# Two transformer-like layers on one core: the long convolution's transforms regrouped by batch and by parity of time, and the bias tables in one buffer

## The reference

```python
xz = einsum('bld,ed->bel', hidden_states, W_in); x, z = split(xz, 2, axis=1)
x  = silu(conv_b + sum_j conv_w[:, j] * xp[:, :, j:j + Lq])      # 4 taps, 256 channels
y  = irfft(rfft(x, 2*Lq) * rfft(k_ssm, 2*Lq))[..., :Lq]          # k_ssm has 512 taps
y  = (y + x * D_skip) * silu(z)
out = einsum('bhl,dh->bld', y, W_out)
...
ctrl = einsum('th,tho->to', hidden, w2) + b2                     # b2 = expert_b2[chosen expert]
```

## Time and profile before

| | |
|---|---|
| three executions | 460.07, 460.67, 460.44 us, median 460.44 |
| the profiled execution | 460.52 us |
| its span, first to last instruction | 458.7 us |
| mean granted TensorE clock | 0.969 |
| PE busy | 420.9 us (92%) |
| PE weight loads busy | 211.1 us (46%) |
| DVE busy | 330.3 us (72%) |
| ACT busy | 190.6 us (42%) |
| DMA moved | 7.27 MB, mean 16 GB/s |

### The profile page before, as it was taken

The page is one execution under the profiler, slowest core; times in us unless marked ns, Lnnn a source line. Parts: engine busy times, 40 slices in busy tenths (PEclk is TensorE's granted clock), DMA queues, the critical chain, the costliest instruction groups (busy, mean ns, idle before and its releaser), DMA issues.

```text
span 458.7 us, 4175 instructions
## 1 busy us (share of the span) xinstructions
PE 420.9 (92%) x1398; PEld 211.1 (46%) x1398; DVE 330.3 (72%) x680; ACT 190.6 (42%) x314; POOL 21.8 (5%) x37
## 2 busy tenths in 40 slices
PE   4792987979999999999999999999999999999992
PEld 1341564655765365344644443433734433343361
DVE  4999898889973994597988674695553863274565
ACT  1343568443136412446143445344037526324441
POOL 0010203011000000000000000000000000000001
PEclk9896999979999999999999999999999999999997
DMA  6300000040000000000000000000000000000001
GB/s 220 150 1 0 1 1 0 2 149 2 1 0 1 1 0 0 1 0 1 1 1 0 1 0 23 0 1 1 0 1 0 24 0 1 1 0 0 1 0 46
DMA packets 5148, 7.27 MB, mean 16 GB/s; under 512 B 1075, under 2 KB 4232, under 8 KB 4872
## 3 DMA queue, kind: packets, MB, share of 16 engines
q1 hardware_dynamic: 3968, 4.80, 3.0%
q10 hardware_dynamic: 1160, 2.21, 1.4%
HBM read 5.95 MB, written 1.05 MB: 15 GB/s over the span
## 4 chain that ended last, share of the span: by engine, by line
PE 72%; DVE 6%; ACT 3%; issue 1%; POOL 1%; POOLq 0%; DVEq 0%
PE ring L1239 23%; PE ring L1217 8%; PE ring L1234 5%; PE timebank L274 5%; PE bankA L200 4%; PE ring L1219 4%; PE specbank L262 3%; PE ring L1247 3%; PE ring L1254 2%; PE ring L1258 2%; PE bankA L274 2%; PE ring L1261 2%; PE bankA L262 1%; PE ring L1265 1%; PE ring L1256 1%; PE ring L1262 1%
## 5 line engine op out<-in xcount | busy, mean ns | idle before, releaser
L1239 PE MATMUL ring<-hm,wc 128*128 128x512 f32 (+1 forms) x252 | 108.6, 581 | 0.0
L1239 PEld LDWEIGHTS ring<-hm,wc 128*128 128x128 f32 x252 | 46.1, 190 | 61.0 <-issue 52.8
L1445 DVE SCALAR_TENSOR_TENSOR hm<-xtm,cst,h 128x512 f32<-128x512 bf16 x48 | 33.4, 747 | 6.0 <-ACT h L1353 6.0
L200 PE MATMUL bankA<-wconv,h2w 128*128 128x256 f32 x128 | 34.9, 423 | 0.0
L1367 ACT ACTIVATE gts<-ring 128x512 f32<-128x512 f32 (+1 forms) x18 | 9.9, 550 | 52.3 <-PE ring L1239 52.3
L1353 ACT ACTIVATE h<-ring,vec 128x512 f32<-128x512 f32 x32 | 21.9, 687 | 17.0 <-PE ring L1219 14.9
L200 PEld LDWEIGHTS bankA<-wconv,h2w 128*128 128x128 f32 x128 | 25.7, 210 | 5.6 <-issue 2.0
L1534 DVE SCALAR_TENSOR_TENSOR f2e<-hl,f2e 128x512 f32<-128x512 f32 (+1 forms) x9 | 5.7, 632 | 27.2 <-ACT hl L1398 27.2
L1234 PE MATMUL ring<-hm,wc 64*128 64x512 f32 (+1 forms) x84 | 22.9, 621 | 0.4 <-DVE hm L1445 0.4
L1364 ACT ACT_TABLE_LOAD x8 | 10.3, 1283 | 28.4 <-PE ring L1239 28.4
L274 PE MATMUL timebank<-cst,abc 128*128 128x256 f32 x96 | 21.2, 379 | 0.0
(11 more groups left out here) (264 smaller groups left out, 762.5 us busy)
## 6 DMA issues: line engine op xcount, KB each, us to landing
wc<-in_w_c SPq DMA_DIRECT2D x1, 1664.0 KB
cst<-in_const ACTq DMA_DIRECT2D x1, 1096.0 KB
out<-xall SPq DMA_DIRECT2D x8, 128.0 KB, 1.9
wc<-in_x_feat SPq DMA_DIRECT2D x1, 768.0 KB, 13.0
bconv<-in_bcast SPq DMA_DIRECT2D x1, 512.0 KB, 7.6
wc<-in_k_time ACTq DMA_DIRECT2D x1, 512.0 KB
wc<-in_x_feat ACTq DMA_DIRECT2D x1, 256.0 KB, 3.7
wa<-in_w_a SPq DMA_DIRECT2D x1, 256.0 KB, 3.5
```

What stands on the lines that cost most here:

```text
L200: ins = pe.matmul(at, h2w[:, n, h * P + tap:h * P + tap + P], wconv[:, tap, :], start=False, stop=(h == HALVES - 1 and tap == TAPS - 1))
L1239: ins = pe.matmul(dst[:, at], wc[:, w:w + P], hm[:, seat(j, made + g - 1), at], start=False, stop=(g == PAIRS - 1))
L1445: dve.scalar_tensor_tensor(hm[:, seat(j, k), :], picked, cst[:, C_EG + g:C_EG + g + 1], h[:, g, :], ALU.is_equal, ALU.mult).then_inc(S["hm ...
```

## The change

1. **Forward unit.** It is now one batch and the whole spectrum. Time is split by parity (even and odd times) and not in halves; `h2w`, the window that feeds the short convolution, is stored by parity for it. The low frequencies (even numbers e = 0) and the mirrored ones (e = 1) share blocks of cosines and sines up to a sign, so the constant table shrinks from 2192 to 1677 columns. A unit is 8 products of 256 columns.
2. **Inverse unit.** Its output is also by parity: 16 products of 128 columns in place of 8 of 256. `gate` puts the two parities back in order of time as it reads `zs` and writes `ys`.
3. **Products on DVE.** The same elements for one batch and the whole spectrum. Two explicit waits on DVE's own earlier results (`Z_ready`) are added.
4. **Lists that are empty.** `FOLDED` and `UNFOLDED` are empty tuples, so `keep_odd`, the branch in `spectra` and those in `products_now` and `inverse_half` issue nothing.
5. **Bias tables.** One float32 buffer of 88 rows of 384 holds the experts' bias twice (rows 0 to 23 and 64 to 87) and the convolution's at rows 32 to 34. It is loaded by one transfer and split once, at the start. The second split, the copy by DMA and PE's wait for it are gone.
6. **Small moves.** `project_gate` reads `h2T` and not the window, so the window's copy no longer waits for the gates' products. The filter is loaded in rows of 512 elements. POOL sets the ones.

```diff
         def forward_half(pe, c, b, bank, ahead=0):
-            after(pe, prod_done, 2 * c + e - ahead)
-            for ri in range(2):
-                for kh in range(HALVES):
-                    ins = pe.matmul(banks[ri][:, :].rearrange("p (b c) -> p b c", b=BATCH), cst[:, C_FWD + kh * 2 * WIN + (2 * ri + e) * P:][:, 0:P],
-                                    xtm[:, c, kh:kh + HALVES + 1:HALVES, :], start=(kh == 0), stop=(kh == HALVES - 1))
+            after(pe, prod_done, 2 * c + b - ahead)
+            for e in range(2):
+                for ri in range(2):
+                    at = bank[:, e, ri * INNER:(ri + 1) * INNER]
...
+                    for par in range(2):
+                        ins = pe.matmul(at, block_of(C_FWD, par, e, ri), xtm[:, c, b * HALVES + par, :], start=(par == 0), stop=(par == 1))
             ins.then_inc(fwd_done, 1)
...
         def inverse_half(pe, c, cc, dst):
             pe.wait_ge(Z_ready, 4 * (c + 1))
             for b in range(BATCH):
-                for e in range(2):
-                    for ri in range(2):
-                        ins = pe.matmul(dst[:, b * WIN:(b + 1) * WIN], z[:, e, at, b * INNER + cc * P:b * INNER + (cc + 1) * P],
-                                        cst[:, C_INV + (2 * ri + e) * WIN:][:, 0:WIN], start=(e == 0 and ri == 0), stop=(e == 1 and ri == 1))
+                for par in range(2):
+                    at = dst[:, (2 * b + par) * P:(2 * b + par + 1) * P]
...
+                    for e in range(2):
+                        for ri in range(2):
+                            ins = pe.matmul(at, z[:, e, ri if c == 0 else 1 - ri, cols], block_of(C_INV, par, e, ri),
+                                            start=(e == 0 and ri == 0), stop=(e == 1 and ri == 1))
...
         def products_late(dve, c, b, bank):
+            dve.wait_ge(Z_ready, 2 * (2 * c + b + 1))
+            after(dve, inv_done, CC * c)
...
         def gate(dve, c, cc, src):
             dve.wait_ge(inv_done, CC * c + cc + 1)
-            dve.tensor_tensor(ys[:, cc, :], src[:, :], zs[:, c, cc, :], ALU.mult).then_inc(gate_done, 1)
+            timed = lambda a: a.rearrange("p (b s a) -> p b a s", b=BATCH, a=2)
+            dve.tensor_tensor(timed(ys[:, cc, :]), src[:, :].rearrange("p (b a s) -> p b a s", b=BATCH, a=2), timed(zs[:, c, cc, :]), ALU.mult).then_inc(gate_done, 1)
...
                 act.dma_start(hT[:, :, 1:1 + WIN], x_feat[:, :, 0:WIN]).then_inc(first_in, 16)
-                act.dma_start(cstb[:, :], consts).then_inc(consts_in, 16)
-                act.dma_start(rowf[:, :], rows.partition_broadcast(3)).then_inc(row_in, 16)
-                for part in range(3):
-                    act.dma_start(bef[part * EXPERTS:(part + 1) * EXPERTS, :], biasE).then_inc(consts_in, 16)
-                act.dma_start(kt[:, :, :], k_time.rearrange("(b p) c -> p b c", p=P)).then_inc(b_in, 16)
+                act.dma_start(biasf[:, :], biases).then_inc(row_in, 16)
+                act.dma_start(kt.rearrange("p (d a) c -> p d (a c)", a=2), k_time.rearrange("(d p a) c -> p d (a c)", p=P, a=2)).then_inc(b_in, 16)
...
-                        after(act, piece_done, (c - 2) * PIECES)
-                        act.activation(h2w[:, :, :], h2T[:, :, ds((c - 2) * WIN, TAPS - 1 + WIN)], ACT.Copy).then_inc(window_placed, 1)
+                        if c > 2:
+                            act.wait_ge(piece_done, (c - 3) * PIECES + BATCH)
+                        act.activation(h2w[:, :, :, :], h2T[:, :, ds((c - 2) * WIN, TAPS + WIN)].rearrange("p b (i q) -> p b q i", q=2), ACT.Copy).then_inc(window_placed, 1)
...
                         rounded(c - 1)
-                        split(bef[:, :], be2split[0:3 * EXPERTS, :], cst[:, C_PM:C_PM + 3], late_split)
                         residual_end(c - 1)
...
-                sp.wait_ge(late_split, 1)
-                sp.dma_start(be2split[HID:HID + 3 * EXPERTS, :], be2split[0:3 * EXPERTS, :]).then_inc(S["biases_doubled"], 16)
```

More of the change, by code:

```diff
@@ L111, in constants @@
     c[:, C_E24] = EXPERTS - np.arange(P) % EXPERTS
-    c[:, C_RANK:C_PM] = EXPERTS - np.arange(EXPERTS)
-    for part in range(3):
[L114 to L117, removed]
+    c[:, C_RANK:C_ALL] = EXPERTS - np.arange(EXPERTS)
+    return c
 class Steps:
@@ L175, in after, with two_layers @@
         eng.wait_ge(sem, count)
-def two_layers(nc, x_tok, x_feat, vecs, bias8, rows, bcast, biasE, w_a, w_b, k_time, d_skip, w_c, w64, w32, const, consts, out):
+def two_layers(nc, x_tok, x_feat, vecs, bias8, bcast, biases, w_a, w_b, k_time, d_skip, w_c, w64, w32, const, out):
     ds = bass.ds
@@ L255, in two_layers @@
         bsteps = Steps(None, b_steps)
[L257 to L264 removed]
+        part = lambda c, b: abc[:, c % 3, :, :, b * INNER:(b + 1) * INNER]
@@ L300, in products_now @@
+        def products_now(dve, c, b, bank, between=None, ready=False):
+            s = bsteps
+            s.eng = dve
+            if not ready:
+                spectra(dve, c, b, bank)
+            xr, xi = real(bank), imag(bank)
+            now, last = part(c, b), part(c - 1, b)
+            after(dve, Z_ready, 2 * (2 * c + b))
+            after(dve, b_steps, s.base + s.n)
             if c == 0:
-                s.go(dve.tensor_tensor(both(now), x2(xr), taps2(e, 0), ALU.mult))
+                s.go(dve.tensor_tensor(now, x2(xr), taps2(0), ALU.mult))
@@ L327, in products_late @@
-        def products_late(dve, c, e, banks):
+            if c == 0 and c not in UNFOLDED:
+                dve.tensor_tensor(now[:, :, 0, :], now[:, :, 0, :], tt[:, :, 0, :], ALU.subtract).then_inc(Z_ready, 1)
+                dve.tensor_tensor(now[:, :, 1, :], now[:, :, 1, :], tt[:, :, 1, :], ALU.add).then_inc(Z_ready, 1)
+                return
+            s.go(dve.tensor_tensor(now[:, :, 0, :], now[:, :, 0, :], tt[:, :, 0, :], ALU.subtract))
+            s.link(dve.tensor_tensor(now[:, :, 1, :], now[:, :, 1, :], tt[:, :, 1, :], ALU.add))
@@ new lines, in products_now @@
+            if c not in UNFOLDED:
+                dve.wait_ge(inv_done, CC * c)
+                dve.tensor_tensor(last[:, :, 1, :], now[:, :, 0, :], last[:, :, 1, :], ALU.subtract).then_inc(Z_ready, 1)
+                dve.tensor_tensor(last[:, :, 0, :], now[:, :, 1, :], last[:, :, 0, :], ALU.add).then_inc(Z_ready, 1)
+                return
+            whole = now
+            if c > 0:
+                whole = tt
+                s.go(dve.tensor_tensor(tt[:, :, 0, :], now[:, :, 0, :], last[:, :, 1, :], ALU.subtract))
+                s.link(dve.tensor_tensor(tt[:, :, 1, :], now[:, :, 1, :], last[:, :, 0, :], ALU.add))
@@ L329, in products_late @@
+            dve.tensor_tensor(last[:, 0, :, :], whole[:, 0, :, :], whole[:, 1, :, :], ALU.add).then_inc(Z_ready, 1)
+            dve.tensor_tensor(last[:, 1, :, :], whole[:, 0, :, :], whole[:, 1, :, :], ALU.subtract).then_inc(Z_ready, 1)
+        def products_late(dve, c, b, bank):
             if c == CHUNKS - 1:
@@ L944, in two_layers @@
             ring3, ring0 = psum("ring3"), psum("ring0")
-            Xb = [psum(f"specbank{i}") for i in range(2)]
             ring1, ring2 = psum("ring1"), psum("ring2")
@@ L1670, in col @@
         return c
+    biases, masks = np.zeros((R_ALL, CTRL), np.float32), np.zeros((R_ALL, 3), np.float32)
+    for part in range(3):
+        for at in (part * EXPERTS, HID + part * EXPERTS):
+            biases[at:at + EXPERTS], masks[at:at + EXPERTS, part] = f["e_expert_b2"], 1.0
+        biases[R_CONV + part, 0:INNER], masks[R_CONV + part, part] = f["m_conv_b"].ravel(), 1.0
     vecs = np.concatenate([col(f["a_time_decay"]), col(f["a_time_first"]), col(f["a_time_mix_key"]), col(f["a_time_mix_value"]),
```

238 lines of the change are left out of this document (130 added, 108 removed).

## The result

The changed kernel takes 461.55 us (median of ten runs, 460.67 to 461.99) against 460.14 us for the kernel before in the same rounds (ten, 459.24 to 460.67). The ratio is 1.0032, interval 1.0022 to 1.0042: 1.4 us slower. The prediction was 461.5 us.

A forecast was written before the change was run, and what follows sets the result against it. The prediction took DVE's chain as the bound up to some 96 us and PE's stream after. 0.84 + 0.17 + 0.1 = +1.1 us on the profiled 460.52 us, less 0.08 us to the median, gave 461.5 us; range 460.3 to 463.2 us.

The forecast's parts named there:

- Inverse units: Eight units on PE's path, each 32 records of 128 columns at 111 ns instead of 16 of 256: +0.84 us.
- longer runs do not hold 111 ns: Rival: PE's longer runs of 128 columns are slower; at 130 ns a record 4.9 us more, 466.4 us; chance 0.05.
- every load uncovered: Rival: 192 ns for each of PE's added weight loads is paid in full, +36.9 us, 498 us; chance 0.01.
- Forward units: Seven units on PE's path, each 16 records of 256 columns instead of 8 of 512: +0.17 us.
- The likeliest rival: No change: 0.20 us at the head of five forward units goes, 460.5 us; chance 0.30, smaller terms included.
- Products on DVE: Same elements per instruction, new waits hidden under PE's stream: 0, or 6 x 0.1 us if uncovered.
- Transfers at the start: The 135 KB bias table competes with `wa`, which starts everything: +0.1 us, between 0 and 0.35.
- the table gets in the way of `wa`: Rival at the start: table delays `wa` or lands after 6.9 us; further +0.3 to +0.5 us, 461.9 us; chance 0.12.
- First split grown: DVE's split at the start grows from 3.06 to 3.82 us, with 0.67 us left before `ksb`: cost 0.
- Gates, window's copy: Steps over every second float32 cost 0; rival that they cost double, +1.5 us, 463.0 us, chance 0.10.
- Second split removed: DVE's 3.82 us from 105.17 us go, but PE, busy from 95.86 us on, does not wait there: gain 0.
- Slow stretch: PE's clock 0.50 from 96 us stays; rival that it goes saves about 3.2 us, 458.3 us, chance 0.05.

The follow-up runs named there:

- experiment 1: Changed kernel with its inverse products back at 256 columns, both parities side by side: 460.67 us, ratio 1.0019 to the kernel before.
- experiment 4: Kernel before with each inverse product of 256 columns cut into two of 128: 461.14 us, ratio 1.0024.
- Experiment 7: Kernel before with each inverse product of 256 columns cut into four of 64: 489.69 us, ratio 1.0637.
- experiment 5: Changed kernel with two unread float32 products of 512 columns keeping PE busy in turn 4: 460.51 us, ratio 1.0004 to the kernel before.
- experiment 6: Kernel before with two unread float32 products of 512 columns keeping PE busy in turn 4: 459.20 us, ratio 0.9981.
- experiment 11: Changed kernel with 256-column inverse products, bias table behind `wa` on SyncE's queue, two unread PE products in turn 4: 458.59 us, ratio 0.9974 to the kernel before.
- experiment 8: Changed kernel with the second split's eight DVE instructions back in turn 4, result unused: 462.17 us, ratio 1.0041 to the kernel before.
- experiment 3: Changed kernel with the bias table behind `wa` on SyncE's queue and the filter waiting for `wa`: 461.29 us, ratio 1.0029 to the kernel before.
- experiment 12: As experiment 11, plus seven unread products of 512 columns on PE in turn 1: 458.06 us, ratio 0.9957 to the kernel before.

## Why the prediction was right, and where it wasn't

- **Inverse units** (forecast +0.84): +0.93 us by the four pairs, 0.23 each. Right; the mechanism, a record's price by its width on PE's path, is shown by experiments 1 and 4 from both sides. The 111 ns of the 16-record row hold for 64 and 128 records. The rival "longer runs do not hold 111 ns" is out, and so is every load uncovered: the trace does not bear out the strict reading of the overlap rule that the prediction weighed. Experiment 7 adds what the prediction did not know: of 256, 128 and 64 columns, 128 is the narrowest that is still nearly free. The Trainium skill's page "TensorE: Matmul & The Clock Gate" (LDWEIGHTS) gives a load by its columns alone, divided by 1.2 per ns; as an estimate by that, 107 ns for 128. The float32 floor of 111 ns agrees within 4%; the bf16 row at 55 ns a record is shorter than this formula gives.
- **Forward units** (+0.17): +0.02 each, +0.12 us. Right, but the prediction counted seven on the path and five behind products of a part of the array; the chain of both kernels has six and four. The likeliest rival, that the 0.20 us at the head of five units would go, did not happen: 3.65 against 3.45 us.
- **Products on DVE** (0): right. From the first complex product of turn 4 to the end of the rounding, where all of it is in the chain, DVE takes 10.2 us in experiment 5 (94.17 to 104.33) and in experiment 6 (95.36 to 105.51), so the regrouping and its waits cost nothing there.
- **Transfers at the start** (+0.1, stated bounds 0 and 0.35): 0.45 us in the first profile, 0.21 to 0.74 us in six profiles with the table beside `wa`, four of them above 0.35. **This is the term that failed**, and its upper bound with it. The prediction priced 135 KB at the best rate in sight, 389 GB/s, and hoped that most of it would fall behind `wa`. The rates of the windows do not bear out a sum of bytes: by 5.0 us the engines had moved only some 68 KB more than before (699 against 631 KB, each window's rate by its 0.5 us), though `wa` landed 0.45 us later, and from 3.0 to 3.5 us they moved less, at 158 and not 285 GB/s. In experiment 11, with the table behind `wa`, they had moved 728 KB by then, and `wa` landed at 4.80. So it is the table's place beside `wa` that costs; how it does so is open, and so is why 0.74 us was reached in one run. The rival "the table gets in the way of `wa`" (0.12), a further 0.3 to 0.5 us, is what occurred in about half of the profiles. Its other half did not occur: the table was there when DVE wanted it at 6.72 us.
- **First split grown** (0): right. It ended with 0.60 us to spare before the scan.
- **Gates, window's copy** (0, up to +1.5): 0.68 to 0.69 us for a gate, as before, and 0.68 for the copy, which moves 520 and not 518 elements (0.64 before). The rule that two hits in a 16-byte line suffice (Trainium skill, "SBUF — State Buffer", Door 1) now agrees with a number: a step of 8 bytes costs at most 0.04 us in 0.64 on ACT and less than 0.01 us on DVE.
- **Second split removed** (0): right in the time, but the cover that the prediction named, PE busy from 96 us on, rests on the slow stretch. When that is short or gone, DVE is 0.15 to 0.27 us late (experiments 8 and 6). The removal may give back up to that in such runs.
- **Slow stretch** (the same, rival at 0.05 and 458.3 us): it began at 96 us, as forecast, but its end varies from run to run between about 99.5 and 103 us. Were it gone, 1.0 us would come back by the medians of experiments 5 and 6, and 1.7 us by the trace in the kernel that the rival priced, not 3.2: its price left out that DVE's chain is next.
- **What the prediction left out.** It put all of the time up to 96 us on DVE and held that work on PE costs nothing there. In turn 1 that is wrong: DVE's norm follows the filter's transform on PE, whose end moves by more than 1 us with the half-clock stretch around it. That term has no part in the sum, and it is as large as the loss that was forecast.
- **Sum.** Widths +1.05 us and a start of +0.21 to +0.74 are +1.3 to +1.8; measured are +1.4 us (1.0 to 1.9 by the interval). The end of the transform in turn 1 and the length of the slow stretch at 96 us move single runs by more than 1 us each; how often each length occurs in the runs without a profile is not known, so the rest of this sum is not shown. That 461.5 us was met within 0.1 us is partly luck: the change cost 1.4 and not 1.1 us, and the kernel before ran at 460.14 and not at the 460.44 us that the forecast started from. The profiled pair alone, +0.15 us, would have taught the wrong lesson.

## What to carry to other kernels

Where PE's stream is the path, cutting these float32 products from 256 to 128 columns cost 3 to 4%, and to 64 columns doubled it: look for a row of the width you are going to before pricing it by its columns. Price even a small transfer issued beside the one that starts everything at its full size and more; to issue it right behind delayed the first scan by at most 0.2 us (experiments 3, 11 and 12: 10.94 to 11.05 us against 10.89), and to hold it back until the other had landed cost 4.4 us, as an in-order engine waited for it. When two profiles differ by less than a slow stretch of the clock can vary, split both chains at common points before reading the difference, look at more than two profiles, and before pricing a stretch ask which engine is next.

## What the runs showed that was not expected

- A float32 record with a load of 128 columns takes 99 to 111 ns for 8, 64 and 128 moving columns alike; in bf16 the same form takes 55 ns.
- The granted clock of one program was 0.50 until before 100 us in one execution and until about 103 us in another, with PE's work ahead of it equal (0.66 of 2 us at 94 to 96 us in both). Nothing here shows what sets its end. In the profile of experiment 4, of the old layout, it ended before 100 us too. That PE's idling ahead is what brings it on is supported by experiments 5, 6 and 12.
- The first stage's end hung on one PE transform 44 us earlier: 44.00 to 44.06 us from its end to the transposes of turn 4 in twelve profiles, while its end moved from 49.75 to 51.15 us.
- A 135 KB transfer delayed the transfer beside it by 0.21 to 0.74 us, and issued only at 4.78 us it needed 6.8 us to land itself.
